# Turning q1 by DMA, b2 by matmul, and activation functions grouped by four tiles in an attention and FFN kernel

## The reference

```python
# x (32,128,512), ctx (32,128,512), mask (32,128), w1 (2048,512), w2 (512,2048)
n = layernorm(x)
s = where(mask, n @ ctx.T / sqrt(512), -1e30)
x = x + softmax(s) @ ctx
h = silu(bitlinear(layernorm(x), w1, b1))
h = gelu(h)
h = layer_norm(h, ln_g, ln_b)
return x + bitlinear(h, w2, b2)
# bitlinear(v, w, b): v is divided by its root mean square, scaled per row so that its
# largest magnitude is 127, and rounded; w is divided by its mean magnitude, rounded and
# clipped to -1..1; then v @ w.T with both scales back, + b
```

## Time and profile before

| | us |
|---|---|
| median of 3 runs | 489.99 (489.21 to 490.1) |
| the profiled execution | 488.48 |
| its span, first to last instruction | 486.7 |
| table loads on ScalarE | 48 of 1.283, and one for the first weight sum |
| DMA transposes | 32 |

### The profile page before, as it was taken

How to read it: one execution, slowest core, us unless ns; L and a number is a source line. 1 busy time by engine, 2 the same in 40 slices (tenths; PEclk the granted TensorE clock), 3 DMA queues, 4 the chain that set the end, 5 groups by cost and what they waited for, 6 DMA issues and landing times. The chain is left out here.

```text
span 486.7 us, 6714 instructions
## 1 busy us (share of the span) xinstructions
PE 413.9 (85%) x1876; PEld 192.9 (40%) x1876; DVE 431.0 (89%) x682; ACT 386.6 (79%) x493; POOL 384.6 (79%) x468
## 2 busy tenths in 40 slices
PE   0564989867999999899989998999999989996377
PEld 0442344323444544354535443455345423332122
DVE  1898599999799999999999999999999799898951
ACT  2553498799799998989898998999899999999400
POOL 0156396979899999989998999899989999994650
PEclk9989799987899999999999999999999999999669
DMA  8989622402435764466546573547444432155065
GB/s 341 377 276 302 260 102 95 130 24 86 93 103 118 201 179 110 108 174 187 137 108 170 154 176 88 149 156 171 101 106 143 102 73 65 44 108 127 24 141 141
DMA packets 93780, 69.95 MB, mean 144 GB/s; under 512 B 70312, under 2 KB 70320, under 8 KB 92976
## 3 DMA queue, kind: packets, MB, share of 16 engines
q1 hardware_dynamic: 93744, 69.52, 50.8%
HBM read 44.31 MB, written 8.39 MB: 108 GB/s over the span
## 5 line engine op out<-in xcount | busy, mean ns | idle before, releaser
L444 PE MATMUL acc<-w2q,q2T 128*128 128x512 bf16 x512 | 122.7, 389 | 9.1 <-DMA q2T<-hid 9.0
L420 PE MATMUL z<-w1q,q1T 128*128 128x512 bf16 x512 | 126.3, 391 | 0.0
L882 DVE SCALAR_TENSOR_TENSOR hid<-hid,rstd,beta 128x2048 f32<-128x2048 f32 x32 | 75.8, 2369 | 4.6 <-POOL rstd L702 4.6
L537 ACT ACTIVATE hid<-z,zs 128x1024 f32<-128x1024 f32 x64 | 70.5, 1106 | 11.5 <-PE z L420 10.8
L444 PEld LDWEIGHTS acc<-w2q,q2T 128*128 128x128 f16 x512 | 48.6, 100 | 70.4 <-issue 12.3
L873 DVE SCALAR_TENSOR_TENSOR hid<-hid,nmu,gain 128x2048 f32<-128x2048 f32 x32 | 76.3, 2385 | 0.0
L420 PEld LDWEIGHTS z<-w1q,q1T 128*128 128x128 bf16 x512 | 45.9, 100 | 76.6 <-issue 33.4
L887 DVE TENSOR_REDUCE am<-hid 128x1 f32<-128x2048 f32 x32 | 72.7, 2272 | 0.0
L715 POOL TENSOR_SCALAR hid<-hid,kq 128x2048 int16<-128x2048 f32 x32 | 63.1, 1970 | 4.3 <-DVE kq L898 4.2
L561 ACT ACTIVATE junk<-hid 128x2048 bf16<-128x2048 f32 x32 | 60.9, 1905 | 5.6 <-DVE hid L882 4.7
L554 ACT ACTIVATE junk<-hid,gsum 128x2048 bf16<-128x2048 f32 x32 | 63.9, 1996 | 0.2
(11 more groups left out here) (99 smaller groups left out, 680.8 us busy)
## 6 DMA issues: line engine op xcount, KB each, us to landing
ctxT<-in_ctxT_dram SPq DMA_DIRECT2D x32, 256.0 KB, 3.9
xs<-in_x_dram SPq DMA_DIRECT2D x32, 256.0 KB, 3.8
xT<-in_xT_dram SPq DMA_DIRECT2D x32, 256.0 KB, 3.8
ctx<-in_ctx_dram SPq DMA_DIRECT2D x32, 256.0 KB, 3.2
out_dram<-xs SPq DMA_DIRECT2D x32, 256.0 KB, 2.5
hid<-in_w1T_dram SPq DMA_DIRECT2D x4, 1024.0 KB, 8.0
hid<-in_w2T_dram SPq DMA_DIRECT2D x4, 1024.0 KB, 9.4
gain<-in_g_dram SPq DMA_DIRECT2D x1, 1024.0 KB, 9.5
```

What stands on the lines that cost most here:

```text
L420: mm = pe.matmul(z_ps[h][:, c * CH:(c + 1) * CH], q1T[:, t % 4, k * P:(k + 1) * P], w1q[:, k, f0:f0 + CH], start=False, stop=(k == DC - 1))
L444: mm = pe.matmul(acc[t % 2][:, :], q2T[:, t % 2, c * P:(c + 1) * P], w2q[:, c, :], start=False, stop=(c == FC - 1))
L537: act.activation(hid[:, t % HR, half(h)], z_ps[h][:, :], ACT.Silu, scale=zs[:, t:t + 1]).then_inc(s_silu[h], 1)
L882: dve.scalar_tensor_tensor(out=hh, in0=hh, scalar=rstd[:, t:t + 1], in1=beta[:, :], op0=ALU.mult, op1=ALU.add).then_inc(s_l, 1)
```

## The change

What it does:

- q1 is rounded by GpSimd to 16-bit whole numbers with an offset of 128 (`round_q1`), and a DMA transpose issued by SyncE turns it (`transpose_q1`). TensorE's four block transposes and ScalarE's copy go.
- What the offset adds to either product is taken back by rows of the same matmul that brings b1 or b2: `fold_w1` and `fold_w2` sum the weights once, `rows1` and `rows2` have 128 rows (b parts in rows 0 to 17, weight sums in 32 to 63), and `brows` the matching factors of a tile. For each step s one transpose turns the factors of the first product of tile s and of the second product of tile s-6 (`turn_factors`, LAG = 6), and VectorE copies them (`copy_factors`).
- b2 comes by that matmul; `add_b2` on GpSimd goes. The bias matmul comes last in the first product and first in the second.
- x1's mean comes from the sum that `add_readout` makes on the way, and its variance from a ScalarE square (`square_x1`); its two statistics steps on VectorE go. `softmax` is one VectorE instruction, after a GpSimd step that prepares the mean's part (`mean_term`).
- Scales are made for two tiles at a time, and several move from GpSimd to VectorE.
- The order of every engine is written out anew, tile by tile at both ends and in a loop over groups of four between them. Attention of tiles t+4 to t+7 stands as one block after the first products of tiles t to t+3. exp, silu and gelu are each taken for the four tiles of a group before the next function. TensorE has a wait for the previous user of a bank ahead of each step. The x ring has 12 buffers instead of 16.
- At the beginning attention of tiles 0 to 3 comes before the weights, and w1 and w2 are partly clamped by a conversion to int32 (`whole_w1`, `whole_w2`), two VectorE steps instead of three, or two behind one ScalarE step.

The core of the diff:

```diff
             def transpose_q1(t):
-                wait(pe, s_q1T, t)
-                ...
-                for c in range(DC):
-                    pe.transpose(q1T_ps[:, c * P:(c + 1) * P], q1[:, c * P:(c + 1) * P, 0], ident_h[:, :])
-                pe.wait_ge(s_bsp, 4 * (t // 2 + 1))
-                pe.transpose(brows_ps, bcols[:, t, :], ident_b[:, :]).then_inc(s_q1Tp, 1)
+                sp.wait_ge(s_q1, t + 1)
+                wait(sp, s_z[0], t - 3)
+                wait(sp, s_z[1], t - 3)
+                sp.dma_start(q1T[:, t % 4, :, :].bitcast(I16), q1[:, t % 3, :], transpose=True).then_inc(s_q1T[t % 4], 16)
+            def turn_factors(s):
+                b = s - LAG
+                ...
+                wait(pe, s_o, b - 1)
+                wait(pe, s_brow, s)
+                pe.wait_ge(s_bsp[3], s + 1)
+                turned_ps = acc[max(b, 0) % 2][0:2 * ROWS, 0:P // 2].bitcast(BF16)
+                pe.transpose(turned_ps, bcols[:, s, :, :].rearrange("p a r -> p (a r)"), ident_b[:, :]).then_inc(s_turned, 1)
             def second_product(t, h):
+                s = t + LAG
                 if h == 0:
                     wait(pe, s_o, t - 1)
-                    pe.matmul(acc[t % 2][:, :], less2, w2sum, start=True, stop=False)
+                    pe.wait_ge(s_brow, s + 1)
+                    pe.matmul(a, brows[:, s % 4, :], rows2[:, :], start=True, stop=False)
 # TensorE, one pass of the loop
+            for t in range(4, 28, G):
+                turn_factors(t + 2)
+                first_product(t + 2, 0), (t + 2, 1); turn_factors(t + 3); first_product(t + 3, 0), (t + 3, 1)
+                pe.wait_ge(s_centred, t + 4)
+                column_sums(t + 4)
+                second_product(t - 4, 0), (t - 4, 1)
+                pe.wait_ge(s_csum, t // 2 + 3)
+                scores(t + 4); second_product(t - 3, 0)
+                pe.wait_ge(s_centred, t + 5)
+                scores(t + 5); second_product(t - 3, 1)
+                pe.wait_ge(s_centred, t + 6)
+                column_sums(t + 6)
+                turn_probs(t + 4); turn_probs(t + 5); readout(t + 4); scores(t + 6); readout(t + 5)
+                scores(t + 7); turn_probs(t + 6); readout(t + 6); turn_probs(t + 7); readout(t + 7)
+                turn_factors(t + 4); second_product(t - 2, 0); first_product(t + 4, 0)
+                turn_factors(t + 5); first_product(t + 4, 1); second_product(t - 2, 1)
+                first_product(t + 5, 0); second_product(t - 1, 0), (t - 1, 1); first_product(t + 5, 1)
 # ScalarE, one pass
+            for t in range(4, 28, G):
+                square_x1(t + 3); silu(t, 1); silu(t + 1, 0); square_l(t - 2); silu(t + 1, 1)
+                silu(t + 2, 0); silu(t + 2, 1); square_l(t - 1); silu(t + 3, 0); silu(t + 3, 1)
+                gelu(t); gelu(t + 1); variance(t); copy_sums(t + 4); variance(t + 1); gelu(t + 2); gelu(t + 3)
+                exp_scores(t + 4); exp_scores(t + 5); copy_probT(t + 4); copy_probT(t + 5); copy_sums(t + 6)
+                variance(t + 2); exp_scores(t + 6); square_x1(t + 4); copy_probT(t + 6); square_x1(t + 5)
+                exp_scores(t + 7); copy_probT(t + 7); variance(t + 3); square_l(t); square_x1(t + 6)
+                square_l(t + 1); silu(t + 4, 0)
 # VectorE, one pass
+            for t in range(4, 28, G):
+                copy_factors(t + 2); gained(t - 1); normed(t - 1); copy_factors(t + 3); x_stats(t + 4)
+                norm_absmax(t - 1); x_stats(t + 5); q2_scale(t - 2, 2); out_scale(t - 2, 2); x_stats(t + 6)
+                gained(t); softmax(t + 4); x_stats(t + 7); normed(t); softmax(t + 5); gained(t + 1)
+                prob_sum(t + 4); norm_absmax(t); add_readout(t + 4); prob_sum(t + 5); softmax(t + 6)
+                x1_absmax(t + 4); add_readout(t + 5); prob_sum(t + 6); softmax(t + 7); x1_absmax(t + 5)
+                q1_scale(t + 4, 2); add_readout(t + 6); z_scale(t + 4, 2); invert_factors(t + 4, 2)
+                output(t - 4); prob_sum(t + 7); output(t - 3); copy_factors(t + 4); add_readout(t + 7)
+                normed(t + 1); gained(t + 2); x1_absmax(t + 6); norm_absmax(t + 1); copy_factors(t + 5)
+                x1_absmax(t + 7); q2_scale(t, 2); q1_scale(t + 6, 2); out_scale(t, 2); z_scale(t + 6, 2)
+                normed(t + 2); invert_factors(t + 6, 2); norm_absmax(t + 2); output(t - 2); output(t - 1)
 # VectorE, softmax and readout
-                dve.scalar_tensor_tensor(out=score[:, t % 4, 0:P], in0=csum[:, t // 2 % 2, t % 2, :], scalar=nm1[:, t:t + 1],
-                                         in1=score_ps, op0=ALU.mult, op1=ALU.add).then_inc(s_centred, 1)
-                dve.tensor_reduce(nmax[:, t:t + 1], score[:, t % 4, :], AX_X, ALU.max, negate=True).then_inc(s_nmax, 1)
-                dve.tensor_scalar(nbias[:, t:t + 1], nmax[:, t:t + 1], rs1[:, t:t + 1], None, ALU.mult).then_inc(s_nb, 1)
+                dve.tensor_tensor_reduce(out=score[:, t % 4, 0:P], in0=corr[:, t % 4, :], in1=score_ps, scale=nrs1[:, t:t + 1],
+                                         scalar=FLOOR, op0=ALU.add, op1=ALU.min,
+                                         accum_out=nbias[:, t:t + 1]).then_inc(s_centred, 1)
```

More of the change, by code:

```diff
@@ new lines, in _ @@
+            silu(3, 1)
+            gelu(0)
+            gelu(1)
+            variance(0)
+            copy_sums(4)
+            variance(1)
+            gelu(2)
+            gelu(3)
+            exp_scores(4)
+            exp_scores(5)
+            copy_probT(4)
+            copy_probT(5)
+            copy_sums(6)
+            variance(2)
+            exp_scores(6)
+            square_x1(4)
+            copy_probT(6)
+            square_x1(5)
+            exp_scores(7)
+            copy_probT(7)
@@ new lines, in _ @@
+            x_stats(0)
+            split_bias()
+            x_stats(1)
+            x_stats(2)
+            softmax(0)
+            x_stats(3)
+            softmax(1)
+            prob_sum(0)
+            weight_sum(0, 1)
+            add_readout(0)
+            prob_sum(1)
+            softmax(2)
+            x1_absmax(0)
+            add_readout(1)
+            prob_sum(2)
+            weight_sum(0, 3)
+            softmax(3)
+            weight_sums_total(0)
+            x1_absmax(1)
+            q1_scale(0, 1)
@@ new lines, in _ @@
+            weight_scale(0)
+            add_readout(2)
+            z_scale(0, 1)
+            q1_scale(1, 1)
+            whole_w1(0)
+            invert_factors(0, 1)
+            z_scale(1, 1)
+            weight_sum(1, 1)
+            clamp_w1(1)
+            invert_factors(1, 1)
+            prob_sum(3)
+            copy_factors(0)
+            whole_w1(2)
+            clamp_w1(3)
+            add_readout(3)
+            x1_absmax(2)
+            copy_factors(1)
+            x1_absmax(3)
@@ new lines, in _ @@
+            q1_scale(2, 2)
+            weight_sum(1, 3)
+            weight_sums_total(1)
+            z_scale(2, 2)
+            invert_factors(2, 2)
+            weight_scale(1)
+            copy_factors(2)
+            whole_w2(0)
+            clamp_w2(1)
+            copy_factors(3)
+            whole_w2(2)
+            x_stats(4)
+            x_stats(5)
+            x_stats(6)
+            clamp_w2(3)
+            gained(0)
+            softmax(4)
+            x_stats(7)
+            normed(0)
@@ new lines, in _ @@
+            softmax(5)
+            gained(1)
+            prob_sum(4)
+            norm_absmax(0)
+            add_readout(4)
+            prob_sum(5)
+            softmax(6)
+            x1_absmax(4)
+            add_readout(5)
+            prob_sum(6)
+            softmax(7)
+            x1_absmax(5)
+            q1_scale(4, 2)
+            add_readout(6)
+            z_scale(4, 2)
+            invert_factors(4, 2)
+            prob_sum(7)
+            copy_factors(4)
+            add_readout(7)
@@ new lines, in _ @@
+            copy_factors(30)
+            gained(27)
+            normed(27)
+            copy_factors(31)
+            norm_absmax(27)
+            q2_scale(26, 2)
+            out_scale(26, 2)
+            gained(28)
+            normed(28)
+            gained(29)
+            norm_absmax(28)
+            invert_factors(32, 2)
+            output(24)
+            output(25)
+            copy_factors(32)
+            normed(29)
+            gained(30)
+            norm_absmax(29)
+            copy_factors(33)
@@ new lines, in _ @@
+            q2_scale(28, 2)
+            out_scale(28, 2)
+            normed(30)
+            invert_factors(34, 2)
+            norm_absmax(30)
+            output(26)
+            output(27)
+            copy_factors(34)
+            gained(31)
+            normed(31)
+            copy_factors(35)
+            norm_absmax(31)
+            q2_scale(30, 1)
+            out_scale(30, 1)
+            q2_scale(31, 1)
+            invert_factors(36, 1)
+            out_scale(31, 1)
+            output(28)
```

1638 lines of the change are left out of this document (1113 added, 525 removed).

## The result

The changed kernel takes 524.14 us (median of 4 runs, 520.78 to 527.47) against 489.6 for the kernel before beside it (486.93 to 490.1): 1.0717 times, 95% interval 1.0634 to 1.08. Forecast were 506 us and a range of 482 to 520. Slower was right, the size was not. The profiled execution took 527.47 us for a span of 525.7.

A forecast was written before the change was run, and what follows sets the result against it. No engine stood out before: four overlapped, VectorE with least slack. After, the new order's ring sets the pace: beginning 92, six periods of 54.4 (326.4) and end 85.5 give a span of 503.9, so 506 us; range 482 to 520.

The forecast's parts named there:

- Ring (steps 1 to 5): Loop: chain of waits through the in-order queues from F(t,0) to F(t+4,0), 54.4 us per group against 50.96 before.
- step 2: ScalarE's silu, gelus, variances and table loads up to exp(t+4) at 40.1; TensorE idle 3 us for the copied column sums.
- 4: End of attention block: probabilities turned and copied, readouts and their adds in turn, readout(t+7) done at 51.5 us.
- 5: After the readouts: factors made, split, turned and copied by 52.25, S0(t-2) 2.06, so F(t+4,0) starts at 54.4 us.
- The clock rival: Second rival: TensorE's clock falls after the 3 us idle in each group, 1.8 us each, 517 us in all; chance 0.24.
- Table loads: ScalarE: three loads per group instead of six, 1.32 us per load by the trace, 4 us per group back.
- q1 by DMA: q1's transpose moves to DMA: TensorE loses 1.2 us per group; transfer taken as 3 us, hidden for three tiles of four.
- b2: b2 as rows of the second product: 32 additions leave GpSimd, the added matmul rows cost TensorE nothing.
- Beginning and end: F(4,0), tile 4's first product, starts at 92 us (82 to 100); from F(28,0) to the end 85.5 (80 to 90).
- The looser ring: Rival: engines' work sets the loop's pace, 49.7 us per group, 475 in all; chance 0.13.
- the short beginning: Rival: weights clamped as they land, F(4,0) at 80; 483 us with the ring at its lower end, else about 490; chance 0.13.
- the six loads: Rival: squares or copies need own table loads, six per group stay, 1.3x3 us more per group, some 515; chance 0.02.

The follow-up runs named there:

- n_filled: The filled base: m_control plus 29 unused TensorE matmuls per loop pass, put into its idle pieces; 518.42 us, ratio 1.0572.
- f_pe_block: n_filled plus eight unused matmuls ahead of the second half of the first product of each group's third tile; 524.95 us, ratio 1.0748.
- f_sums_first: n_filled with ScalarE's copy of the column sums (t+4) moved ahead of gelu(t); 517.47 us, ratio 1.0608.
- the squares: One more ScalarE square per group: ahead of exp(t+4) on m_control (533.7 us) and on n_filled (522.12), or ahead of a silu on m_control (524.81).
- m_control: Changed kernel with both DMA transposes (q1, q2) written as plain copies of the same bytes; 531.04 us, ratio 1.0873.
- before_onetable: Kernel before the change, its q2 transpose written as a plain copy and gelu computed by silu's function; 483.97 us, ratio 0.9911.
- n_square_silu: m_control plus one more 128x2048 ScalarE square per group, ahead of silu(t+1,1); 524.81 us, ratio 1.0629.
- f_b2_apart: n_filled with b2 added by GpSimd again, the second product starting from a constant, two more TensorE waits; 529.01 us, ratio 1.0807.
- f_onetable: n_filled with gelu computed by silu's function, which drops the table load between silus and gelus; 511.29 us, ratio 1.0468.

## Why the prediction was wrong

- **Ring (steps 1 to 5)**: right at full clock. 54.4 was walked; 54.49 is the one full-clock group of the changed kernel, 54.5 to 54.75 the filled base's. That it agrees to 0.1 is luck in part: from column_sums(t+4) to F(t+4,0) it took 30.86 us (walked 30.3), from there to the next column sums 23.63 (walked 24.1). f_pe_block and f_sums_first put TensorE's block on it and its idle piece of step 2 off it, the squares exp 1 us off it. In the pass from 266 to 320 us of the changed kernel gelu starts at 293.43, exp at 306.66, scores(t+4) after 3.27 idle (said: 3), column sums end at 308.2. That the grouping by four is what closes it follows from the order; no run undid the grouping alone.
- **The step that failed** is 4, with 5 behind it: readout(t+7) and S0 were priced at the full clock's 1.02 and 2.06 us. Four groups of five ran them at 1.2 GHz, 2.05 in place of 1.10 and 3.62 in place of 1.89 by the rows, 2.7 us each, after short idle pieces that step 4 itself has between its times. With the falls behind step 2's idle piece the loop took 18.2 us more than forecast. The loop's part of the sum had no term for the clock.
- **The clock rival** had the mechanism and nearly the price for its own place (1.8 said, 2.3 measured on the way to column_sums(t+6) and 1.7 in the period), but placed the fall only behind step 2's 3 us, in every group, where two in five had it (four in m_control), and not behind step 4's short pieces, where four had it. Its 517 was short of 524 for that, and at 0.24 it stood behind a forecast that needed the clock to stay up. n_filled, with the clock up in the loop, has a span of 510.3: F(4,0) at 94.81, six periods of 55.0 and 85.4 us behind, so 2.8, 3.7 and -0.1 more than forecast. The Trainium skill (TensorE: Matmul & The Clock Gate, A second HAM failure mode: psum-queue depth-cycling) has a kernel whose clock oscillates because TensorE often idles briefly between groups of matmuls; the trace agrees, with pieces of 0.46 to 0.98 us ahead of the fall. I had drawn only on that page's default state.
- **Table loads**: right. 24 are left (26 said), 1.28 us each; in before_onetable 19 fewer were worth 2.1 us.
- **q1 by DMA**: hidden, as said, though the sign against it came: the profile names q1T as what ended 5.3 us of TensorE's waits, 3.7 of them ahead of S0. But in the program S0 waits for the copied factors, the output before it and q2T, not for q1T, and it starts 29.14 us behind the column sums in the full-clock group of the changed kernel as in that of n_square_silu, where q1 is a plain copy and the same 0.61 us are put down to the copied factors.
- **Signs**: TensorE's idle time ahead of scores(t+4) (3.27, ended by the copied sums) and VectorE's ahead of gained(t) (7.22 from 292.1 us) came. Of 53 to 56 us between column sums only one period in five did; the clock under 1.00, named as the second rival's sign, stood in the other four.
- **Engines' totals**: VectorE 74% and ScalarE 68% (76% and 70% said), and no gain from it.
- **b2**: costed at nothing on TensorE. It seems to gain some: f_b2_apart.
- **Beginning and end**: 94.97 (92; 98.17 in m_control), 86.1 (85.5). The looser ring, the short beginning and the six loads did not come.

## What to carry to other kernels

Before grouping steps to save table loads, walk the ring that the grouping closes through the in-order queues: a load that lay beside other work is worth little when it goes (2.1 us for 19 of them here), and the idle pieces that the new order opens on TensorE, even those that cost nothing as waits, can be paid at half clock behind them. Price matmuls behind a stretch of short idle pieces at both clocks. When a kernel's time varies with the mean granted clock, fill those pieces in one experiment before arguing about order, and compare periods group by group: the beginnings of two runs of one kernel can differ by as much as the effect.

## What the runs showed of the hardware

- The clock fell after idle pieces of 0.46, 0.98 and 0.46 us (257.4 to 260.8) and was at 1.00 again from 268; the same pieces brought no fall in the group from 120.23. After one idle piece of 3.27 us it fell in two groups of five, in m_control in four. With matmuls without use in these pieces it was at 1.00 in 25 groups of 25, without them in 4 of 25.
- Runs of one kernel differed with the clock, 519.0 us of span at 0.931 and 525.7 at 0.909, and without it, 510.3 at 0.953 and 516.2 at 0.950 (n_filled).
- A switch of activation function costs what its row says: 1.28 us of load, and without one of them on the ring (f_onetable) the period was 1.1 to 1.15 us shorter.
- A GpSimd step of 0.69 us took 4.81 beside two 2048-wide VectorE steps:

```profile
262.23 0.69 POOL L1077 TENSOR_SCALAR xc<-xs,sum 128x512 f32<-128x512 f32 x1
...
264.11 4.81 POOL L1077 TENSOR_SCALAR xc<-xs,sum 128x512 f32<-128x512 f32 x1 [0.35 <-DVE xs L1464]
```

The hold goes both ways: the same VectorE step took 3.24 us beside more GpSimd work, 2.58 beside less, 2.35 elsewhere (303.67 in the changed kernel).
